# A two-layer Mamba kernel with routed experts: the gated rows are halved in fp16 and turned by DMA instead of by TensorE

## The reference

```python
h = x                                   # [8, 512, 256]
for i in range(2):                      # two Mamba2 layers
    res = h
    h = layernorm(h, ln_w[i], ln_b[i])
    z, xBC, dt = split(h @ in_w[i].T)   # 512, 640, 8 columns
    xBC = silu(conv1d(xBC, 4 taps))
    y = scan(xBC, softplus(dt + bias), A) + D * xh      # 8 heads of 64, state 64
    y = y * silu(z)
    y = y * rsqrt(mean(y * y) + eps) * rms_w
    h = y @ out_w[i].T + res
x = layernorm(x + h)
# then top 2 of 8 gated experts over the 4096 rows, hidden size 1024
x = layernorm(x + sum_of_two(w_e * ((silu(x @ w1g_e) * (x @ w1x_e)) @ w2_e)))
```

## Time and profile before

| | us |
|---|---|
| median of 3 runs (lowest, highest) | 1397.85 (1397.28, 1399.97) |
| the profiled execution | 1405.77 |
| its span, first to last instruction | 1403.8 |
| scan part, 41 to 745 us of the span | 704.0 |
| expert part and final sums, from 745 us | 658.8 |

### The profile page before, as it was taken

One profiled execution on the slowest core, in us unless ns is written; L12 is line 12 of the kernel. 1 busy time (PEld: TensorE's weight loads), 2 busy tenths in 40 slices (PEclk: granted clock), 3 DMA queues, 4 the chain that ended last, 5 costly groups with the idle time before them and its releaser, 6 DMA issues. The chain is left out here.

```text
span 1403.8 us, 40595 instructions
## 1 busy us (share of the span) xinstructions
PE 1253.7 (89%) x13192; PEld 1031.3 (73%) x13193; DVE 1143.5 (81%) x2632; ACT 797.6 (57%) x1863; POOL 786.8 (56%) x743
## 2 busy tenths in 40 slices
PE   4889999999999999899978879999999999999990
PEld 2456666666666676667667768999999999999980
DVE  4889999999999999899976886868677867686666
ACT  5666666666766766676634344544545455445446
POOL 3467676666766787687775340707043706170772
PEclk9899999999999999999966989999999999999995
DMA  6213432334443223321225542231514151412554
GB/s 211 81 35 121 135 100 85 111 109 135 136 136 106 96 62 122 108 87 58 91 112 147 141 118 58 67 117 41 146 45 138 42 146 45 137 43 56 150 144 157
DMA packets 120720, 146.63 MB, mean 104 GB/s; under 512 B 47744, under 2 KB 103552, under 8 KB 120512
## 3 DMA queue, kind: packets, MB, share of 16 engines
q1 hardware_dynamic: 109504, 102.15, 24.1%
q0 software_dynamic: 10848, 42.32, 9.7%
q10 hardware_dynamic: 288, 1.19, 0.2%
HBM read 98.83 MB, written 37.47 MB: 97 GB/s over the span
## 5 line engine op out<-in xcount | busy, mean ns | idle before, releaser
L1111 PE MATMUL pe<-arena 128*128 128x128 f16 x3408 | 218.8, 222 | 26.0 <-issue 19.1
L1111 PEld LDWEIGHTS pe<-arena 128*128 128x128 f16 x3408 | 202.5, 99 | 32.6 <-issue 30.7
L1111 PE MATMUL pa<-arena 128*128 128x128 f16 x3408 | 217.7, 221 | 3.1 <-DVE pm L2315 2.5
L1136 PE MATMUL py<-arena 128*128 (+1 forms) x1704 | 199.4, 274 | 5.5 <-issue 3.3
L1111 PEld LDWEIGHTS pa<-arena 128*128 128x128 f16 x3408 | 200.1, 99 | 3.4 <-DVE pm L2315 2.7
L1572 ACT ACTIVATE arena<-pe,arena 128x128 f32<-128x128 f32 x568 | 161.4, 370 | 68.0 <-PE pe L1111 67.5
L1705 DVE SCALAR_TENSOR_TENSOR arena<-pa,arena 128x511 f32<-128x511 f32 (+2 forms) x240 | 178.7, 745 | 11.7 <-ACT arena L1209 5.6
L1136 PEld LDWEIGHTS py<-arena 128*128 128x128 f16 x1704 | 164.5, 98 | 24.8 <-issue 5.0
L1744 DVE TENSOR_TENSOR_SCAN arena<-arena,pe 128x512 f32<-128x512 f32 x128 | 148.8, 1203 | 3.0 <-issue 1.6
L2557 POOL TENSOR_SCALAR arena<-arena 128x1536 f16<-128x1536 f32 (+2 forms) x35 | 45.3, 1295 | 180.7 <-DVE arena L2363 175.3
L833 PEld LDWEIGHTS py<-arena 128*128 128x128 f32 x1024 | 124.0, 197 | 17.4 <-issue 8.5
(11 more groups left out here) (306 smaller groups left out, 2542.1 us busy)
## 6 DMA issues: line engine op xcount, KB each, us to landing
arena<-step_rows SPq DMA_DIRECT2D x64, 512.0 KB, 5.8
arena<-in_w_exp POOLq DMA_DIRECT2D x32, 768.0 KB, 4.9
arena<-queue SPq DMA_DIRECT2D x74, 129.5 KB
answer<-arena SPq DMA_DIRECT2D x71, 128.0 KB, 1.7
arena<-in_x SPq DMA_DIRECT2D x16, 512.0 KB, 6.1
answer<-zeros SPq DMA_DIRECT2D x10, 512.0 KB, 4.8
arena<-h SPq DMA_DIRECT2D x9, 512.0 KB, 6.2
h<-arena SPq DMA_DIRECT2D x8, 512.0 KB, 3.0
```

The source lines that it names most:

```text
L1111: ins = pe.matmul(bank[:, f * P:(f + 1) * P], w_split[:, p, hl, d * 2 * FF + col:d * 2 * FF + col + P], x_hl[:, r, x, d * P:(d + 1) * P], ...
L1136: ins = pe.matmul(py[:, 0:D], a[:, b, f, :], part(p, hl, W1N + f * D, D), start=(half == 0 and n == 0), stop=(half == 1 and n == len(passe ...
```

## The change

The turning of g leaves PE. ACT writes the high half of g by rows (g_high, new), POOL the low half by rows (g_low, moved from DVE; in final and the epilogue it stays on DVE), both into a new buffer g_hl, and SP issues one DMA transpose for each chunk (turn_g, new), which turns eight blocks of 128x128 fp16 into gT. The scale 2 (SG), which the copy out of pt used to apply, is applied to x (chunk_a) and taken out again in squares. Bank pt belongs to chunk_a alone. The product of a unit's last chunk, c[3], moves into the next unit (Chunk(st, -1)), and chunk_d stands later in the orders of PE and ACT. The split of the second expert's weights waits for plan_done, the whole table, and not for rows_done.

```diff
+            def turn_g(u, k):                      # SP
+                n = NK * u + k
+                sp.wait_ge(gl_ready, n + 1)
+                at_least(sp, out_full, n - 1)
+                sp.dma_start_transpose(gT[:, k % 2].rearrange("p a c t -> p (a c) t"),
+                                       g_hl[:, k % 2].rearrange("p a n -> p (a n)")).then_inc(g_turned[k % 2], 16)
...
-            def chunk_c(c):                        # PE
-                pe.wait_ge(g_ready, c.n + 1)
-                pe.wait_ge(pt_free, c.use("o"))
-                for t in range(NCT):
-                    ins = pe.transpose(pt[:, t * P:(t + 1) * P], gk[:, t * P:(t + 1) * P], ident[:, :])
-                ins.then_inc(pt_full, 1)
             def chunk_d(c):
-                pe.wait_ge(pt_free, c.use("o") + 1)
+                pe.wait_ge(g_turned[c.kq], c.turned())
...
-            def chunk_c(c):                        # ACT
-                e.wait_ge(pt_full, c.use("o") + 1)
-                e.activation(gT[:, kq, 0].rearrange("p c t -> p (c t)"), pt[:, :], ACT.Copy, scale=SG).then_inc(gh_ready, 1)
+            def g_high(c):
+                e.wait_ge(g_ready, c.n + 1)
+                at_least(e, g_turned[kq], c.turned() - 16)
+                e.activation(g_hl[:, kq, 0], g[:, kq].rearrange("p h d -> p (h d)"), ACT.Copy).then_inc(gh_ready, 1)
...
-                dve.scalar_tensor_tensor(gT[:, c.kq, 1].rearrange("p c t -> p (c t)"), pt[:, :], SG,
-                                         gT[:, c.kq, 0].rearrange("p c t -> p (c t)"), ALU.mult,
-                                         ALU.subtract).then_inc(pt_free, 1)
+            def g_low(c):                          # POOL; DVE in final and epilogue
+                pool.wait_ge(gh_ready, c.n + 1)
+                pool.tensor_tensor(g_hl[:, c.kq, 1], g[:, c.kq].rearrange("p h d -> p (h d)"), g_hl[:, c.kq, 0],
+                                   ALU.subtract).then_inc(gl_ready, 1)
...
                 if e == 1:
-                    pool.wait_ge(rows_done, 1)
-                if e == 2:
                     pool.wait_ge(plan_done, 1)
```

More of the change, by code:

```diff
@@ L115, in __init__ @@
         self.first, self.last, self.s3, self.before = first, last, s3, before
+        self.before_layer = 0 if isinstance(u, int) and u == NB else layer
         self.epilogue = isinstance(u, int) and u >= MAMBA_UNITS
@@ L943, in plain @@
                 chunk_cb(c[1])
+                chunk_d(Chunk(st, -1))
                 do_fills(st, ["c4"])
@@ L1026, in routed @@
                 chunk_cb(c[4])
-                chunk_d(c[3])
             def final(st):
@@ L1032, in final @@
                 chunk_a(c[1])
+                chunk_d(Chunk(st, -1))
                 chunk_cb(c[1])
                 chunk_s(c[0])
-                chunk_c(c[0])
                 chunk_z(c[1])
@@ L1040, in final @@
                 chunk_y(c[1])
-                chunk_d(c[0])
                 chunk_a(c[2])
@@ L1045, in final @@
                 chunk_z(c[2])
-                chunk_c(c[1])
+                chunk_d(c[0])
                 chunk_s(c[2])
@@ L1485, in final @@
                 chunk_a(c[1])
+                chunk_d(Chunk(st, -1))
                 end_scale(st)
-                chunk_c(c[0])
+                g_high(c[0])
                 h_out(st, 0)
@@ L1963, in first @@
                 taps(st, "c0", ch1)
-                g_low(c[0])
                 weigh(st)
@@ L1973, in first @@
                 next_state(c[1])
-                g_low(c[1])
                 chunk_mix(c[3])
@@ L1980, in first @@
                 scan(c[4])
-                g_low(c[2])
                 next_state(c[2])
@@ L2060, in routed @@
                 scan(c[4])
-                g_low(c[3])
                 chunk_mix(c[4])
@@ L2093, in epilogue @@
                 roots(0, 3, 1)
+                g_low(Chunk(st.before, NK - 1))
                 end_last(st, 0)
                 end_last(st, 1)
-                g_low(Chunk(st.before, NK - 1))
                 end_last(st, 2)
@@ L2716, in plain @@
                 x_d(c[1])
+                g_low(c[0])
                 add_xd(c[1])
@@ L2720, in plain @@
                 x_w(c[2])
+                g_low(c[1])
                 x_dt(c[2])
@@ L2728, in plain @@
                 x_dt(c[3])
+                g_low(c[2])
                 x_d(c[3])
@@ L2733, in plain @@
                 u_low(st.u + 2, st.q, st, "ln0")
+                g_low(c[3])
                 u_low(st.u + 2, st.q, st, "ln1")
```

174 lines of the change are left out of this document (76 added, 98 removed).

## The result

The changed kernel takes 1441.62 us, median of 4 runs (1435.0 to 1443.52), against 1398.91 (1397.28 to 1401.54) in the same comparison. The ratio is 1.0289, 95% interval 1.0257 to 1.0321. The profiled execution took 1440.1 us, its span is 1438.4.

The account below looks back on a forecast made before the run. PE and DVE were taken as nearly full, with late transposes and POOL's g_low binding after the change. 17.5 + 15 - 4 - 5 = +23.5 us, 1421 from the median 1397.85; range 1372 to 1446.

Parts of the forecast that it names:

- part of -4: Units 0, 1, 9 and final have no full burst or no scatters and gain a little: 4 us together.
- the split: In the lead, two DVE instructions no longer run beside POOL's split: 5 us less taken, bounds 0 and 9.
- What is removed: Four transposes a chunk on PE and g_low on DVE: 2.6 and 2.7 us a unit, both given up by 15 units.
- turned for nothing: Rival: every transpose is covered, PE and DVE set the pace; 36 us and 5 of the split, 1357; 12%.
- What is added: POOL gets 60 g_low, 4.6 us a unit; SP gets 64 eight-block transposes, taken as 3.4 us each.
- my 27.8 for the plain loop: Plain unit, from chunk_d c[2] to the next add_x's end: 27.8 us, against 28.8 before.
- Plain units: c[2]'s transpose stands behind the third broadcast: loop 43.2 us, 2.5 more in each of seven units, 17.5 together.
- the burst: SP's store, clearing, load and broadcasts in a plain unit; DMA engines busy at 0.99 from 202.5 to 209.5 us.
- the 2.5 us: Plain unit longer because c[2]'s transpose waits behind the third broadcast: 2.5 us a unit, bounds 0.5 and 4.0.
- A landing 12.8 us behind add_x's end: Landing of c[2]'s transpose from which a plain unit is no slower; the forecast landing was 15.4.
- Routed units: POOL reaches g_low c[0] late and chunk_d c[0] waits: 3.0 us a unit in units 10 to 14, 15 together.
- The clock: Rival: PE, waiting 3 to 5 us in each unit, may lose granted clock in the scan part; 1441 to 1465; 13%.

Follow-up runs that it names:

- the split alone: Kernel before with only the second expert's split waiting for plan_done: 1393.81 us, ratio 0.9953.
- old orders, nothing turned: Kernel before in its own orders, without transposes of g or g_low, products on output weights without waiting, split waiting for the plan: 1366.92 us, ratio 0.9757.
- new orders alone: Changed kernel without g_low and DMA transposes, products on output weights waiting for nothing of g: 1398.10 us, ratio 0.9993.
- The two reorderings tried: Changed kernel with waiting output products later in PE's order (1427.20 us), then also g_low of c[0] and c[1] later on POOL (1414.98 us).

## Why the prediction came out as it did

Forecast 1421 in a range of 1372 to 1446, slower with 0.63; measured 1441.6. The direction and the places of the waits were right; the sum reached only 23.5 of 42.7 us, and two of its terms were far off and nearly cancelled, which was luck. By the stretches of the two traces the terms were:

| stretch | forecast | measured |
|---|---|---|
| plain units 2 to 8 | +17.5 | +12.3 |
| routed units 10 to 14 | +15 | +20.3 |
| units 0, 1 and 9 | part of -4 | +7.7 |
| unit 15 and behind it, with the split | -5, and part of -4 | -5.7 |

And by the medians of the runs above:

| term | forecast | measured | from |
|---|---|---|---|
| the split | -5 | -5.8 | the split alone |
| the turning taken off PE and DVE, with the wait for it | -4 | -26.9 | old orders, nothing turned, against the split alone |
| the new orders | 0 | +31.2 | new orders alone against old |
| POOL's g_low | part of +15 | +22.6 | with and without it |
| the transposes' traffic | 0 | -1.8 | in the noise |
| the wait for them | +17.5, and part of +15 | +22.8 | with and without it |

The rows are the steps of one chain of kernels from the one before to the changed one; they add up to 42.1. Another chain, the waits in the old orders for instance, could give other sizes. The second and third row together are what the removed work gave in the new orders: +4.3 us, where -4 was forecast.

- *What is removed.* Whether PE's order covers the transposes was all that I asked of the new orders. The step that was furthest off is the one that let the removed 5.3 us a unit give next to nothing except in units 0, 1, 9 and final: with the old orders it gives up to 26.9 us. The rival "turned for nothing" (36 us) came nearer to this size. I gave the reordering itself no price, and it is the largest term: +31.2.
- *What is added.* The eight-block transpose issues in 1.23 us and lands after 3.1; I took 3.4, with 1.9 to 2.4 of issue. POOL's g_low takes some 1160 ns (1157 forecast), and POOL is at 40.8 us in a routed unit (41). That it would hold up end_b and end_add I had named, at most 1.2 us a unit, and left inside the bounds; end_b is 0.95 us longer in every plain unit, and my 27.8 for the plain loop has no term for it.
- *Plain units.* c[2] waits for a DMA as forecast, but for 1.1 to 1.9 us and not 3 to 5. Its transpose was not held in SP's queue by the third broadcast: it was issued as soon as g_low was done. Only its landing was late, by some 1.5 us, and taking more than half of that away gained nothing. Forecast 43.2 us a unit; measured 42.4, of which the wait holds 0.7 and g_low 0.9. That these are so near is luck too. Here is the loop in the unit shown above, add_x, chunk_mix c[4], end_b and the next add_x (chunk_d c[2] starts at 349.34):

```profile
334.88 2.00 POOL L2569 TENSOR_TENSOR arena<-arena 128x1024 f32<-128x1024 f32 x1
...
351.36 1.22 DVE L1742 TENSOR_TENSOR arena<-arena,pe 128x1024 f32<-128x1024 f32 x1 [0.75 <-PE pe L806]
...
366.67 3.63 DVE L1709 SCALAR_TENSOR_TENSOR arena<-arena 128x256 f32<-128x256 f32 x4
...
377.44 2.00 POOL L2569 TENSOR_TENSOR arena<-arena 128x1024 f32<-128x1024 f32 x1
```

  From add_x's end (336.88) the transpose has landed after 12.4 us, forecast 15.4, because the third broadcast went out sooner in the burst and landed after 4.6 us and not 6.8. From chunk_d c[2] to the next add_x's end (379.44) it is 30.1, forecast 27.8. A landing 12.8 us behind add_x's end was my point from which a plain unit is no slower, and it was slower: the burst, from which the 2.5 us came, wasn't what made it longer. What was added lies in the 30.1, where I had counted a gain, and without any wait for the transposes a plain unit still takes 41.7 us (291.8 for seven). The Trainium skill (DMA: Bandwidth & Descriptors, section Queues, rings and completion order) says that on each DMA engine descriptors are consumed in ring order. The trace agrees as far as it goes: behind the broadcast the transpose landed 0.86 us after it, and moved ahead of it, it landed about 1 us sooner after its issue. That the two share the engines' bandwidth would look the same; no run separates them.
- *Routed units.* The chain was right in place: g_low behind add_xd, chunk_d c[0] waiting (1.6 to 3.2 us; 1 to 3 forecast). Forecast +3.0 a unit for units 10 to 14; measured +4.1, with +2.6 for g_low and +1.4 for the wait. Unit 9, which I had among those that gain, lost 3.8.
- *The split.* Right in mechanism (3.17 us to 0.39), and in size by the medians of the pair in the kernel before (5.8; 5 forecast). In the traces the lead's first six tiles are 10 to 11 us shorter, so more than the two instructions that I counted gets shorter there. The Trainium skill (SBUF — State Buffer, section SBUF: two separate sides) gives the mutual lock of a GpSimd instruction and a VectorE one with two SBUF inputs; the pair of runs agrees.
- *The clock.* I had it as a rival with 1441 to 1465, and the measured 1441.6 lies in its range as well as in the forecast's own (1403 to 1448). The clock did fall, 30.7 us at its lower level in units 10 to 14 against 6.8 before, but taking half of that away gave 1.7 us there, so in these units it is a small part. In unit 15 it cost some 4 us of the traced execution. Its share in the rest of the scan part is not shown.

## What to carry to other kernels

When a step leaves an engine, price the new order of what remains as a change of its own. A run that keeps the order and drops the work, and one that keeps the new order and drops the work, cost two kernels and separate a gain of up to 27 us from a 31 us loss that a sum over instructions can't see. When work moves to POOL, look at DVE's instructions beside it: here end_b took 3.63 us and not 2.68 in every plain unit. A wait that the profile shows in front of an instruction is no measure of its worth: here removing 0.9 us of wait per plain unit gave nothing, and another wait grew.

The best kernel seen that computes the reference is the one before with only the split moved, 1393.81 us. The old orders with a turning that costs nothing showed 1366.9, so at most 27 us are there to be had; whether a version with DMA transposes in orders nearer to the old ones comes below 1393.8 wasn't tried. The two reorderings tried brought the changed kernel from 1441.6 to 1415.0.

## What was not expected of the hardware

A DMA transpose of eight 128x128 fp16 blocks takes the same issue time on SP as one of four (1.23 against 1.22 us) and 3.1 us to its landing against 2.5. By these two sizes the issue does not grow with the blocks and the landing grows by 0.6 us. And 64 such transposes beside the broadcasts (DMA share in plain units 0.49 against 0.34 without them) cost no measurable time when nobody waits for them.
